# First routed loads asked for from attention step 28, one shared bias folded into the expert biases, gated sums regrouped: an attention and mixture-of-experts kernel on one core

## What is computed

```python
xn  = layernorm(x)                                   # x: 4096 rows (8 x 512) of 256
out = x + attention(xn, k, v) + ffn(xn)
# attention: softmax(xn k^T * scale) v, 1024 keys; scale is taken from rows of xn
# ffn: a shared expert, and 8 routed experts of which each row takes its best 2
shared = gelu(xn @ Wfc_s + bfc_s) @ Wproj_s + bproj_s
probs, idx = top_k(softmax(xn @ Wr), 2); gate = probs / sum(probs)
routed = sum_e gate_e * (gelu(xn @ Wfc[e] + bfc[e]) @ Wproj[e] + bproj[e])
ffn = shared + routed                                # hidden width 1024
```

## Time and profile before

| | |
|---|---|
| median of 3 runs | 823.47 us (821.97 to 823.82) |
| the profiled execution | 822.49 us |
| its span, first to last instruction | 820.6 us |
| TensorE busy | 777.3 us, 95% |
| VectorE, ScalarE, GpSimd busy | 483.1, 440.5, 260.4 us |
| mean granted TensorE clock | 0.988 of full speed |

### The profile page before, as it was taken

One profiled execution on the slowest core, in us unless ns is written; L12 is line 12 of the kernel. 1 busy time (PEld: TensorE's weight loads), 2 busy tenths in 40 slices (PEclk: granted clock), 3 DMA queues, 4 the chain that ended last, 5 costly groups with the idle time before them and its releaser, 6 DMA issues.

```text
span 820.6 us, 21229 instructions
## 1 busy us (share of the span) xinstructions
PE 777.3 (95%) x7222; PEld 662.1 (81%) x7222; DVE 483.1 (59%) x1215; ACT 440.5 (54%) x845; POOL 260.4 (32%) x289
## 2 busy tenths in 40 slices
PE   4999999999999986979999999999999999999996
PEld 3888876767777665868999999989999999888885
DVE  6887858888887792653444344333444433436666
ACT  5655537665559753435655465444455554455551
POOL 5445425556656650662121111112112121110000
PEclk9999999999999997999999999999999999999999
DMA  9533222746566845444422355645454536304446
GB/s 296 193 128 104 84 73 78 259 154 232 203 209 227 332 187 193 131 135 122 158 73 65 116 174 162 203 131 161 160 167 123 191 118 205 100 26 138 125 150 213
DMA packets 65627, 129.29 MB, mean 158 GB/s; under 512 B 12256, under 2 KB 47408, under 8 KB 59168
## 3 DMA queue, kind: packets, MB, share of 16 engines
q1 hardware_dynamic: 59088, 110.77, 42.2%
q0 software_dynamic: 6480, 17.77, 5.7%
HBM read 88.39 MB, written 40.13 MB: 157 GB/s over the span
## 4 chain that ended last, share of the span: by engine, by line
PE 73%; DVE 13%; POOL 5%; issue 4%; DMA 3%; SPq 1%; DVEq 0%; ACT 0%; another core or an unknown queue 0%; POOLq 0%; ACTq 0%
PE ps_h L1321 30%; PE ps_v L1341 30%; PE ps_v L1461 5%; PE ps_h L1393 4%; POOL acc L637 3%; DVE xn L895 3%; PE ps_t L1257 2%; DVE prob L1018 2%; PE ps_t L1407 1%; DVE p_t L1032 1%; DMA tokens_y<-prob,to_i 1%; POOL slots_x L660 1%; DVE acc L1040 1%; DMA b_rows<-in_L_ffn_bfc_s_dram 1%; DVE x_t L845 1%
## 5 line engine op out<-in xcount | busy, mean ns | idle before, releaser
L944 DVE TENSOR_TENSOR h_split<-h,h_split 128x512 f16<-128x512 f32 (+1 forms) x224 | 151.5, 686 | 153.5 <-ACT h_split L751 152.8
L745 ACT ACTIVATE h<-ps_h,b_fc 128x256 f32<-128x256 f32 (+1 forms) x320 | 125.7, 443 | 181.7 <-PE ps_h L1321 181.6
L1321 PE MATMUL ps_h<-x_t,w_split 128*128 128x256 f16 (+1 forms) x1920 | 196.6, 263 | 7.3 <-DVE x_t L1134 7.3
L1321 PEld LDWEIGHTS ps_h<-x_t,w_split 128*128 128x128 f16 x1920 | 172.6, 99 | 26.0 <-issue 8.1
L1341 PE MATMUL ps_v<-w_stage,h_split 128*128 128x256 f16 x1704 | 192.6, 273 | 0.0
L1341 PEld LDWEIGHTS ps_v<-w_stage,h_split 128*128 128x128 f16 x1704 | 165.1, 98 | 18.5
L704 POOL DMA_INDIRECT tokens_y<-prob,to_i x71 | 72.0, 1015 | 309.1 <-DMA tokens_y<-prob,to_i 200.1
L751 ACT CAST h_split<-h 128x512 f16<-128x512 f32 (+1 forms) x224 | 130.7, 584 | 10.1
L745 ACT ACTIVATE h<-ps_h,b_t 128x256 f32<-128x256 f32 x128 | 53.4, 467 | 76.4 <-PE ps_h L1321 76.2
L1461 PE MATMUL ps_v<-v_split,p_t 128*128 128x256 f16 x768 | 90.9, 276 | 0.0
L1321 PE MATMUL ps_h<-x_t,w_shared 128*128 128x256 f16 x768 | 89.4, 278 | 0.0
(11 more groups left out here) (156 smaller groups left out, 665.4 us busy)
## 6 DMA issues: line engine op xcount, KB each, us to landing
w_split<-wpack SPq DMA_DIRECT2D x17, 1024.0 KB, 5.3
w_stage<-wpack SPq DMA_DIRECT2D x17, 1024.0 KB, 5.3
wpack<-w_split SPq DMA_DIRECT2D x8, 1024.0 KB
wpack<-h_split SPq DMA_DIRECT2D x8, 1024.0 KB, 5.0
y_rows<-tokens_y SPq DMA_DIRECT2D x32, 256.0 KB, 3.1
x_split<-slots_x SPq DMA_DIRECT2D x31, 258.0 KB
b_pj<-bias_e SPq DMA_DIRECT2D x40, 128.5 KB, 3.1
w_stage<-in_L_ffn_Wfc_dram SPq DMA_DIRECT2D x4, 1024.0 KB
```

Source lines behind the costliest of these rows:

```text
L745: ins = nc.scalar.activation(h32[:, hc, 0:n], ps_h[:, hc * TILE:hc * TILE + n], ACT.Gelu_apprx_tanh, bias=bias[:, hc:hc + 1], scale=1.0 / WS)
L944: ve.tensor_tensor(h_split[par][:, 1, 2 * b:2 * b + 2, 0:n], h32[:, 2 * b:2 * b + 2, 0:n], h_split[par][:, 0, 2 * b:2 * b + 2, 0:n], ALU.s ...
L1321: ins = mm(ps_h[:, hc * TILE:hc * TILE + cols], wv[:, wl, c, hc * P:(hc + 1) * P], x[:, xl * DC + c, 0:cols], start=n == 0, stop=n == 3 * ...
```

## The change

The weights and tiles of the first two routed steps are asked for at other places of SP's program: from step `u = 28` of the attention loop, behind the store of job 14 and before that of job 15, it waits for the table, the scattered rows and the padding, issues `load_slots` of steps 0 and 1, and after waits for the stores that the weights need issues `load_fc` of step 0. Behind the loop follow `load_fc` of step 1 (which waits for the store of job 13) and, after all stores, `load_pj` of step 0. The functions themselves are moved, with only a wait for `s_bias_e` changed from 32 to 16.

The shared bias `bproj_s` is loaded into 8 partitions in place of 128 (in the space of `b_pj[0]`), `bproj` into the new `b_both`, one GpSimd instruction of 8x256 adds the two, and SP stores the sum as `bias_e`. As the gates of a row add up to 1, this brings the shared bias in with the expert bias. `add_bias` and its wait on VectorE are gone.

The second half of `w_shared[0]` is scaled to its high part by one ScalarE instruction, and its low part comes from VectorE, as in the first half.

The gated sums are divided over the tiles as 5, 5, 5, 5, 4, 4, 4 and 0.

```diff
-        b_pj_s = sb("b_pj_s", [P, D], f32)
+        b_pj_s = b_pj[0][0:EXPERTS, 0:D]
+        b_both = sb("b_both", [EXPERTS, D + 1], f32)
...
-        CONSTS = 16
+        CONSTS = 17
...
-        PER = QT // (SHARED - NA)
+        SUMS = (range(0, 5), range(5, 10), range(10, 15), range(15, 20), range(20, 24), range(24, 28), range(28, 32), ())
...
-            sp.dma_start(b_pj_s[:, :], bproj_s.partition_broadcast(P)).then_inc(s_bpj_in, 16)
+            sp.dma_start(b_pj_s[:, :], bproj_s.partition_broadcast(EXPERTS)).then_inc(s_bpj_in, 16)
+            sp.dma_start(b_both[:, 0:D], bproj).then_inc(s_bpj_in, 16)
             load_x(2)
             wait_ge(sp, s_const, CONSTS)
-            sp.dma_start(bias_e[:, 0:D], bproj).then_inc(s_bias_e, 16)
-            sp.dma_start(bias_e[:, D:D + 1].rearrange("e o -> o e"), iota_e[0:1, :], allow_slow_non_contiguous=True
-                         ).then_inc(s_bias_e, 16)
...
+            wait_ge(sp, s_bias, 1)
+            sp.dma_start(bias_e, b_both[:, :]).then_inc(s_bias_e, 16)
...
+                if u == 28:
+                    wait_ge(sp, s_table, TABLE)
+                    for par in range(2):
+                        wait_ge(sp, s_scat[par], 32 * SHARED)
+                    wait_ge(sp, s_pad, 16 * (EXPERTS + SUB))
+                    load_slots(0, 0, False, first=True)
+                    load_slots(1, 1, True, first=True)
+                    wait_ge(sp, s_bt_out, 16)
+                    for n in range(4):
+                        wait_ge(sp, s_w_out[n], 16 * (EXPERTS // 4))
+                    wait_ge(sp, s_w_out[0], 16 * (JOBS // 4))
+                    load_fc(0, 0, first=True)
+            wait_ge(sp, s_w_out[1], 16 * (JOBS // 4))
+            load_fc(1, 1, first=True)
             for n in range(4):
                 wait_ge(sp, s_w_out[n], 16 * (JOBS // 4))
-            wait_ge(sp, s_bt_out, 16)
-            wait_ge(sp, s_table, TABLE)
-            load_fc(0, 0, first=True)
-            for par in range(2):
-                wait_ge(sp, s_scat[par], 32 * SHARED)
-            wait_ge(sp, s_pad, 16 * (EXPERTS + SUB))
-            load_slots(0, 0, False, first=True)
-            load_slots(1, 1, True, first=True)
-            load_fc(1, 1, first=True)
             load_pj(0, 0, first=True)
...
-                for p in range(g * PER, (g + 1) * PER):
+                for p in SUMS[g]:
...
+            g.iota(b_both[:, D:], pattern=[[0, 1]], base=0, channel_multiplier=1,
+                   allow_small_or_imprecise_dtypes=True).then_inc(s_const, 1)
...
-            def add_bias(i):
-                x = acc[:, i * SUB:(i + 1) * SUB, :]
-                g.tensor_tensor(x, x, b_pj_s[:, :].unsqueeze(1).to_broadcast([P, SUB, D]), ALU.add).then_inc(s_bias, 1)
...
-            wait_ge(pool, s_w0_hi[1], 1)
-            g.tensor_tensor(w_shared[0][:, 2048 + HID:], w_stage[0][:, HID:], w_shared[0][:, HID:2 * HID],
-                            ALU.subtract).then_inc(s_w0_lo[1], 1)
+            wait_ge(pool, s_bpj_in, 32)
+            g.tensor_tensor(b_both[:, 0:D], b_both[:, 0:D], b_pj_s[:, :], ALU.add).then_inc(s_bias, 1)
...
-            wait_ge(pool, s_bpj_in, 16)
-            wait_ge(pool, s_fin, QT)
-            for i in range(SHARED):
-                add_bias(i)
...
-            nc.scalar.mul(w_stage[0][:, HID:], w_stage[0][:, HID:], WS).then_inc(s_w0_sc, 1)
-            act.wait_ge(s_w0_sc, 1)
-            nc.scalar.copy(w_shared[0][:, HID:2 * HID], w_stage[0][:, HID:]).then_inc(s_w0_hi[1], 1)
+            nc.scalar.mul(w_shared[0][:, HID:2 * HID], w_stage[0][:, HID:], WS).then_inc(s_w0_hi[1], 1)
...
-            dve.wait_ge(s_w0_hi[0], 1)
-            ve.scalar_tensor_tensor(out=w_shared[0][:, 2048:2048 + HID], in0=w_stage[0][:, 0:HID], scalar=WS,
-                                    in1=w_shared[0][:, 0:HID], op0=ALU.mult, op1=ALU.subtract).then_inc(s_w0_lo[0], 1)
+            def split_w0_lo(c):
+                dve.wait_ge(s_w0_hi[c], 1)
+                ve.scalar_tensor_tensor(out=w_shared[0][:, 2048 + c * HID:2048 + (c + 1) * HID],
+                                        in0=w_stage[0][:, c * HID:(c + 1) * HID], scalar=WS,
+                                        in1=w_shared[0][:, c * HID:(c + 1) * HID], op0=ALU.mult, op1=ALU.subtract
+                                        ).then_inc(s_w0_lo[c], 1)
+
+            split_w0_lo(0)
             copy_xt(0)
+            split_w0_lo(1)
...
-                    dve.wait_ge(s_bias, SHARED)
                 else:
                     if i > NA + 1:
-                        dve.wait_ge(s_gated, TOP * PER * (i - NA - 1))
+                        dve.wait_ge(s_gated, TOP * SUMS[i - NA - 1][0])
                     evict_shared(i - 1, t - 1)
                     dve.wait_ge(s_ev, 2 * t)
-                    for p in range((i - NA - 1) * PER, (i - NA) * PER):
+                    for p in SUMS[i - NA - 1]:
                         add_routed(p)
-            for p in range(QT - PER, QT):
-                add_routed(p)
```

More of the change, by code:

```diff
@@ L249, in moe_attention_block @@
         s_w0_in = sem2("s_w0_in")
-        s_w0_sc = sem("s_w0_sc")
         s_w0_hi = sem2("s_w0_hi")
@@ L514, in load_pj @@
                 if first:
-                    wait_ge(sp, s_bias_e, 32)
+                    wait_ge(sp, s_bias_e, 16)
                 sp.dma_start(b_pj[par][:, :], bias_e[ds(e, 1), :].rearrange("e n -> (e n)").partition_broadcast(P)
@@ L528, in load_slots @@
                 sp.dma_start(dst, src).then_inc(s_xs_in[par], 16)
+            for u in range(QT):
+                k, phase = u // 3, u % 3
+                i = NA + 1 + k
+                if phase == 1 and i < SHARED:
+                    store_row(i)
+                if u == 0:
+                    load_job(3)
+                for n in range(JOBS):
+                    if u == lo_slot(n, 1) + 1:
+                        store_job(n)
+                        if n + 4 < JOBS:
+                            load_job(n + 4)
+                if u % 4 == 2 and u // 4 + 2 < BATCH:
+                    load_scale(u // 4 + 2)
+                if u == 25:
+                    wait_ge(sp, s_table, PAD_ROWS)
+                    for e in range(EXPERTS):
+                        first_pad = sp.value_load(tab_pad[0:1, e:e + 1], min_val=0, max_val=SPARE - P)
+                        sp.dma_start(rows(slots_x, first_pad, P), zeros[:, :, :]).then_inc(s_pad, 16)
+                if u == 28:
[12 more added lines that the diff above has]
+            load_fc(1, 1, first=True)
             for n in range(4):
                 wait_ge(sp, s_w_out[n], 16 * (JOBS // 4))
-            wait_ge(sp, s_bt_out, 16)
-            wait_ge(sp, s_table, TABLE)
-            load_fc(0, 0, first=True)
-            for par in range(2):
-                wait_ge(sp, s_scat[par], 32 * SHARED)
-            wait_ge(sp, s_pad, 16 * (EXPERTS + SUB))
-            load_slots(0, 0, False, first=True)
-            load_slots(1, 1, True, first=True)
-            load_fc(1, 1, first=True)
             load_pj(0, 0, first=True)
```

19 lines of the change are left out of this document (removed).

## The result

The changed kernel takes 795.42 us (median of 4 runs, 793.99 to 796.73), the one before 822.72 (4 runs, one more than in the table above). The ratio is 0.967, with an interval of 0.964 to 0.969, so 27.3 us are gone. 795.3 was forecast. In a later comparison (`changed_again`, 5 runs against 9) the ratio was 0.970 (0.968 to 0.971), 24.9 us.

The account below looks back on a forecast made before the run. TensorE, 95% busy, was taken as the bound wherever nothing holds it. Gains of 11.7 + 11.2 + 4.5 + 0.3 = 27.7 us gave 794.8 from the profiled 822.49 or 795.8 from the median; forecast 795.3, range 792.8 to 801.

Parts of the forecast that it names:

- 11.7 forecast: Late attention, at `tr2_first`: earlier requests remove TensorE's 9.2 us wait and the slow clock behind it, 11.7 us.
- no cost: SP's queue and first routed weights: moved requests delay nothing; step 0's weights land one to two microseconds before they are wanted.
- sign of being wrong: First routed up-projection: a wait of TensorE at `ps_h` for weights between 323 and 357 would disprove the prediction.
- 5.3 us to landing: Step 0's routed weights: requested at about 302 to 303, taking 5.3 us, landing at 307.3 to 308.3.
- rival of the late weights: First routed step: store of job 15 delays the weights to 312, TensorE stands 2.8 us, 798.1; chance 10%.
- 11.2 forecast: Start of the routed stage, attention's end to step 5's up-projection: 44.08 us becomes 32.88 without `add_bias`, 11.2 us gained.
- late scatters 4.5 us at least: Routed start: lower bound if only the scatters' part comes back, the last of three waits plus slow clock, some 4.5 us.
- rival of the scatters as the bound: First two routed pairs: three scatters take 17.0 against 16.44, losing 1 to 2 us, 796.8; chance 5%.
- 4.5 forecast: Kernel's end: last sums finish before TensorE, span ends at 816.1, a gain of 4.5 us (3.7 to 5.1).
- 0.3 forecast, between -1 and +0.5: Front: second half of `w_shared[0]` ready sooner, 0.3 us gained; the 8x256 addition could make it 1 us late.
- a hold that would have made it -0.2: Front: VectorE's new split held for GpSimd's full 8x256 addition if that starts first, giving -0.2 in place of +0.3.
- two bases: Whole kernel: 27.7 us off the profiled 822.49 gives 794.8; off the median of the runs, 795.8; 795.3 was said.

Follow-up runs that it names:

- changed_again: The changed kernel as it is, timed again beside the kernel before: 795.74 us against 821.09, ratio 0.9697.
- Edit 1: Tiles and weights of the first routed steps requested earlier by SP; alone on the kernel before, 810.10 us against 820.19, ratio 0.9883.
- w_first: Changed kernel with step 0's routed weights requested once `tab_e` is there, ahead of the tile loads: 795.41 us against the changed kernel's 795.74.
- Edit 2: Shared bias folded into the expert biases, `add_bias` gone; alone on the kernel before, 810.54 us against 820.19, ratio 0.9881.
- Edit 3: Gated sums divided 5, 5, 5, 5, 4, 4, 4, 0; alone on the kernel before, 816.38 us against 820.19, ratio 0.9954.
- Edit 4: Second half of `w_shared[0]` split by ScalarE and VectorE; alone on the kernel before, 818.72 us against 820.19, ratio 0.9987.
- front_order: Changed kernel with VectorE normalizing and splitting tile 1 before ranking tile 0: 794.41 us against 819.23 for the kernel before, ratio 0.9690.
- e2_bias: Kernel before with only the shared bias folded into the expert biases, no `add_bias`: 810.54 us against 820.19, ratio 0.9881.

## Why the prediction was right

**Edit 1, 11.7 forecast.** 11.6 in the attention step; alone, 11.0 up to the first routed step with the late weights taken off, and 9.6 us (7.7 to 11.5) timed. The request of the tiles was right too: 301.83, in an execution 1.3 us late as a whole. What failed is the "no cost" of the weights. I gave them one to two us of room and named any wait of TensorE for them as a sign of being wrong, and it waits 0.3 to 0.5 us in seven of the eight traces with this order of requests. The size that was off is the 5.3 us to landing: the load took 6.1 to 6.6 us in the six traces that record it, and 4.9 before. With 5.3 it would have been there at 309.8, 0.8 before TensorE wanted it (310.56). So the rival of the late weights came true in small, not with 2.8 us. Which transfer beside it slows the load is open: in `w_first` the request is earlier and also ahead of the tiles, so it does not tell the time of the request from its neighbours.

**Edit 2, 11.2 forecast.** 11.2 in steps 1 to 5 of the trace, 9.8 us (8.4 to 11.2) timed alone. The size was right because it was read as a distance between two marks of TensorE. What I said of the mechanism was not: I gave VectorE's hold a share and the late scatters 4.5 us at least. The late scatters alone are enough for all of it. I had read their price off the third wait, which the first two had shortened. Held off alone, the first scatter costs 7.2 us when it starts 19.5 us behind attention and 10.6 us at 24.6, where it starts at 9.6 in the changed kernel; the slow matmuls are in that. The rival of the scatters as the bound did not come: in the changed kernel GpSimd waits for VectorE between them, once 7.41 us before the scatter at 351.65.

**Edit 3, 4.5 forecast.** 4.7 in the trace, 3.8 (2.5 to 5.0) timed alone. The end came 3.1 us behind the last matmul, 3.3 was forecast. The five-sum tiles cost TensorE nothing.

**Edit 4, 0.3 forecast, between -1 and +0.5.** The first up-projection starts 0.3 us sooner in the trace after, as forecast, and 0.3 to 1.0 sooner in the six traces of that front. The bounds were too narrow for what follows: the traces of the same front differ by 4 us at step 29. The up-projection of tile 1 starts between 22.70 and 24.05, and its 48 matmuls take 5.40 to 7.07 us; from there to step 29 the traces differ by another 1.6, which was not followed. A sum of durations does not hold that. Alone the edit gains 1.1 us (0.2 to 1.9), which does not rule out 0.3. The 8x256 addition took 0.72 us and not the 0.5 at most that I scaled from a wider one, without harm: it ended at 14.41, before `inv_std` of tile 1 had its input. It started at 13.69, behind VectorE's second split (done at 11.74), so the two never met, and a hold that would have made it -0.2 had no occasion.

**The sum.** 27.7 forecast, 25.7 in the trace, 27.3 and 24.9 us timed. The forecast of 795.3 lies 0.1 from the median, and that is luck: the terms are not that good, and the two timed gains differ by 2.4 us. The 2 us between sum and trace (late weights, front) and the choice of 795.3 between two bases cancel in part. The gaps add, as the product of the four ratios (0.971) shows within its noise.

## What to carry to other kernels

Where one engine is the bound, read each gap as the distance between two of its marks and subtract what lies between at its own rate: for the first two edits that gave 11.7 and 11.2 us before anything ran, and the trace has 11.6 and 11.2, though the mechanism behind the second gap was read wrongly. Work for a helper engine that waits for the end of a stage and stands in its queue ahead of the next stage's first hand-off can cost the stage much of its length, even if nothing reads its result soon: here 23 us of work cost some 11. The same work in pieces behind the hand-offs cost 3 us by the trace. A longer wait at one place is not yet a loss: the bias fold alone made TensorE wait 4.7 us in the front and left it 0.5 us later at step 29. And before a small gain is sought, see how far traces of one and the same code lie apart: here 4 us in the front.

## What was not expected of the hardware

After a wait of about a microsecond TensorE's clock sometimes falls a level (2.4 to 1.2 GHz) and sometimes does not. In the changed front the up-projection of tile 0 is followed by two short waits, for the transposes and for the router. Two executions with the same code up to there, `changed_again` and `w_first`, TensorE in order of time:

```profile
12.13 5.50 PE L1318 MATMUL ps_h<-x_t,w_shared 128*128 128x256 f16 x36
...
20.71 0.62 PE L1254 MATMUL ps_t<-ident_h,x_split 128*128 128x128 f16 x8 [1.64 <-DVE x_split L903]
...
22.70 6.65 PE L1318 MATMUL ps_h<-x_t,w_shared 128*128 128x256 f16 x48
```

```profile
12.23 6.41 PE L1319 MATMUL ps_h<-x_t,w_shared 128*128 128x256 f16 x36
...
20.95 0.62 PE L1255 MATMUL ps_t<-ident_h,x_split 128*128 128x128 f16 x8 [0.87 <-DVE x_split L904]
...
22.92 5.40 PE L1319 MATMUL ps_h<-x_t,w_shared 128*128 128x256 f16 x48
```

In the first the 36 matmuls take 5.50 us, TensorE waits 1.64 and the next 48 take 6.65, with a granted clock of 0.50 (1.2 GHz) from 22.7 to 25.0 us and 1.00 from 27.0 on. In the second the 36 take 6.41, the wait is 0.87 and the 48 take the full-rate 5.40, at 1.00 throughout. In the three traces of the table that have a wait there and 5.40 behind it, the wait is 0.87 or less, but `front_order` has 0.64 and 7.07 (with a longer wait for the router, 1.48 against 1.1). In these three and in the trace before the 36 matmuls took 6.41 to 6.92; where they took 5.45 to 6.28 the 48 were slow, save in `e2_bias` (6.01). So a faster start did not make a shorter front: TensorE gets ahead of VectorE, waits for it, and then often runs at half rate. That the one follows from the other is my reading of the table, and no run was made to test it; what decides it in a single execution stays open.
